# Attention stage written out lap by lap: scores two sequences ahead, value products between score steps, split of the maxima on GpSimd, second LayerNorm applied on ScalarE, two row buffers

## The reference, cut to what matters

```python
h = _layernorm(x, ln1_g, ln1_b)
qkv = h @ w_qkv + b_qkv
q, k, v = jnp.split(qkv, 3, axis=-1)          # each [B, S, H=16, DK=8]
scores = jnp.einsum('bqhd,bkhd->bhqk', q, k) / np.sqrt(DK)
attn = jax.nn.softmax(scores, axis=-1)
o = jnp.einsum('bhqk,bkhd->bqhd', attn, v).reshape(B, S, D)
x = x + o @ w_o + b_o
h = _layernorm(x, ln2_g, ln2_b).reshape(B * S, D)
logits = h @ gate_w + gate_b
topv, topi = jax.lax.top_k(logits, TOPK)
```

## Time and profile before

| | |
|---|---|
| median of three runs | 776.5 us (772.96 to 779.0) |
| the profiled execution, its own time | 773.37 us |
| its span, first to last instruction | 771.5 us |
| mean granted clock of TensorE | 0.901 of full speed |
| busy in the span: TensorE, DVE, POOL, ScalarE | 79%, 66%, 57%, 49% |

### The profile page before, as it was taken

How to read it: one execution, slowest core, us unless ns; L and a number is a source line. 1 busy time by engine, 2 the same in 40 slices (tenths; PEclk the granted TensorE clock), 3 DMA queues, 4 the chain that set the end, 5 groups by cost and what they waited for, 6 DMA issues and landing times. The chain is left out here.

```text
span 771.5 us, 19028 instructions
## 1 busy us (share of the span) xinstructions
PE 607.2 (79%) x5634; PEld 494.0 (64%) x5634; DVE 512.3 (66%) x1558; ACT 379.7 (49%) x796; POOL 436.2 (57%) x524
## 2 busy tenths in 40 slices
PE   3999936999992887379999899999931499999950
PEld 1556625989991554246777666667621499999950
DVE  2655544766762889546789678788654378778735
ACT  1543403655560444337777767767511355556520
POOL 2477761766776576342436575576476055666650
PEclk9999977999995699759999999999975699999985
DMA  5921146766754279313443353355214798888519
GB/s 166 255 69 48 52 101 170 216 199 199 220 154 125 74 217 272 121 38 96 91 111 91 81 134 86 85 130 118 40 40 98 240 292 257 244 253 243 174 40 325
DMA packets 97817, 115.03 MB, mean 149 GB/s; under 512 B 16128, under 2 KB 77600, under 8 KB 97632
## 3 DMA queue, kind: packets, MB, share of 16 engines
q1 hardware_dynamic: 82224, 92.36, 44.0%
q0 software_dynamic: 9088, 18.76, 7.7%
q10 hardware_dynamic: 6448, 3.20, 1.7%
HBM read 80.75 MB, written 33.53 MB: 148 GB/s over the span
## 5 line engine op out<-in xcount | busy, mean ns | idle before, releaser
L403 POOL DMA_INDIRECT dispatch_rows<-row,index x128 | 127.5, 996 | 86.3 <-DVE index L384 51.0
L765 POOL DMA_INDIRECT expert_rows<-fo,to x78 | 84.0, 1077 | 67.0 <-DVE fo L1804 53.5
L1501 DVE TENSOR_REDUCE mneg<-ps 128x4 f32<-128x512 f32 x128 | 86.8, 690 | 42.3 <-PE ps L1619 40.2
L765 POOL DMA_INDIRECT expert_rows<-eo,to x78 | 75.0, 962 | 48.5 <-ACT eo L858 25.6
L1593 ACT ACTIVATE prob<-ps 128x512 f32<-128x512 f32 x128 | 76.3, 598 | 51.4 <-PE ps L1628 45.7
L738 DVE CAST xh<-psT 128x256 fp32r<-128x256 f32 x78 | 33.1, 425 | 73.2 <-PE psT L706 71.5
L1619 PE MATMUL ps<-km,qp 96*128 96x512 f32 x128 | 58.4, 459 | 23.3 <-POOL km L1453 17.0
L1793 PE MATMUL psO<-wb,fh 128*128 128x128 f32 x624 | 75.9, 275 | 0.0
L1793 PEld LDWEIGHTS psO<-wb,fh 128*128 128x128 f32 x624 | 73.1, 192 | 0.0
L756 PE MATMUL psA<-xh,wh 128*128 128x256 f32 (+1 forms) x234 | 73.0, 312 | 0.0
L1453 POOL TENSOR_SCALAR km<-kp,const 96x512 fp32r<-96x512 f32 x32 | 52.6, 1644 | 24.8 <-DMA kp<-qk_parts 18.7
(11 more groups left out here) (200 smaller groups left out, 1549.5 us busy)
## 6 DMA issues: line engine op xcount, KB each, us to landing
wb<-in_W1b SPq DMA_DIRECT2D x39, 578.0 KB
w<-in_W SPq DMA_DIRECT2D x39, 304.0 KB
qk_parts<-qk SPq DMA_DIRECT2D x8, 1024.0 KB, 5.0
qp<-qk_parts SPq DMA_DIRECT2D x48, 128.0 KB, 3.2
kp<-qk_parts SPq DMA_DIRECT2D x48, 128.0 KB, 3.5
qm<-qk_parts SPq DMA_DIRECT2D x192, 32.0 KB
xs<-dispatch_rows SPq DMA_DIRECT2D x39, 130.0 KB
xt<-dispatch_rows SPq DMA_DIRECT2D x39, 130.0 KB
```

Source lines behind the costliest of these rows:

```text
L403: pool.indirect_dma_start(out=m.xbuf, out_offset=bass.IndirectOffsetOnAxis(ap=r.index[b][:, c:c + 1], axis=0), in_=r.row[b][:, c // TOPK, ...
L765: pool.indirect_dma_start(out=m.ybuf, out_offset=bass.IndirectOffsetOnAxis(ap=to[b][:, a:a + 1], axis=0), in_=out[b][:, a, :], in_offset=N ...
L1501: ins = nc.vector.tensor_reduce(mneg[p][:, g, :], ps1[:, g % 2, :].rearrange("p (j k) -> p j k", j=4), AX_X, ALU.max, negate=True)
```

## The change

`attention` and its `post_*` steps are written out as straight code for all sequences, in laps s from 0 to 45; the work of a group n lies in fixed laps after 4n (`group(s, after)`).

- Scores: eight for sequences 0 and 1 come first, then lap s holds `score(s + 2)` beside `shift(s)`; `mix(s - 1)` and `total(s - 1)` are cut in two halves each, one behind each group g. `turn_max(s + 1)` stands behind g = 1, `project(s - 2)` behind g = 2.
- Masks of the keys: three sequences are made first, then lap s ends with `mask_k(s + 3)` on ScalarE, behind the fourth exponential. There are still two `km` buffers, and three of `qp` and `kp`.
- The split of the maxima (`part_max`) is done by POOL, at the head of a lap.
- The second LayerNorm: DVE makes -mean times rstd (`post_centre`), ScalarE applies it, between the third and the fourth exponential of its lap.
- The router's steps on DVE are cut in single operations between the maxima. The last groups use the same banks as the others. The two row buffers alternate (n % 2), and two rows' DMAs go out in each of the laps 4n + 10 to 4n + 13, four at a time before.
- The semaphore `spare` is joined with `tails`.

The diff, cut to its core; what it takes out of the streams is printed above.

```diff
+def post_centre(q, dve, n):
 
     dve.wait_ge(q.rooted, n + 1)
-    wait(dve, q.turned, n)
+    wait(dve, q.normed, n)
+    q.m.nc.vector.scalar_tensor_tensor(out=q.offset[:], in0=q.mv[:, :, 0], scalar=-1.0, in1=q.rstd[:],
+                                       op0=ALU.mult, op1=ALU.mult).then_inc(q.centred, 1)
+
+
+def post_normalise(q, act, n):
+
+    act.wait_ge(q.centred, n + 1)
+    wait(act, q.turned, n)
     for t in range(GT):
-        ins = q.m.nc.vector.tensor_scalar(q.norm[:, t, :], post_stream(q, n, t), q.mv[:, t, 0:1],
-                                             q.rstd[:, t:t + 1], ALU.subtract, ALU.mult)
+        ins = q.m.nc.scalar.activation(q.norm[:, t, :], post_stream(q, n, t), ACT.Identity,
+                                       bias=q.offset[:, t:t + 1], scale=q.rstd[:, t:t + 1])
...
+        LAPS = SEQS + 14
+
+        def group(s, after):
+
+            n, rest = divmod(s - after, GT)
+            return n if rest == 0 and 0 <= n < GROUPS else None
...
+                for k in range(PAIRS):
+                    if k >= 2:
+                        if k >= PAIR_BUFFERS:
+                            sp.wait_ge(shifted, HG * 2 * (k - PAIR_BUFFERS + 1))
+                        load_pair(m, sp, k, k % PAIR_BUFFERS)
+                    if k < 2:
+                        sp.wait_ge(zeroed[k], 1)
+                    else:
+                        sp.wait_ge(shifted, HG * 2 * (k - 1))
...
+                def part_max(s):
+                    p = s % 2
+                    pool.wait_ge(maxed, HG * (s + 1))
+                    wait(pool, turned, s - 1)
+                    x = xm[p][:]
+                    hi, lo = (bass.AP(x.tensor, x.offset + w, [list(x.ap[0]), [32, HG], [130, 4]]) for w in range(2))
+                    nc.gpsimd.tensor_copy(hi.bitcast(F32R), mneg[p][:]).then_inc(link, 1)
+                    pool.wait_ge(link, s + 1)
+                    nc.gpsimd.tensor_tensor(lo, mneg[p][:], hi, ALU.subtract).then_inc(parted, 1)
...
+                mask_k(0)
+                mask_k(1)
+                nc.gpsimd.memset(qm[1][:].bitcast(F32), 0.0).then_inc(zeroed[1], 1)
+                for b in range(2):
+                    nc.gpsimd.memset(xm[b][:], 0.0)
+                    nc.gpsimd.memset(vb[b][:], 0.0).then_inc(cleared, 1)
+                nc.gpsimd.memset(post.minus_half[:], -0.5)
+                pool.wait_ge(cleared, 2)
+                part_max(0)
+                mask_k(2)
+                for s in range(LAPS):
+                    if s + 1 < SEQS:
+                        part_max(s + 1)
+                    if s + 3 < SEQS:
+                        mask_k(s + 3)
+                    if s < SEQS:
+                        spread_v(s)
+                    n = group(s, 6)
+                    if n is not None:
+                        post_root(post, pool, n)
+                    for part in range(GT):
+                        n = group(s, 10 + part)
+                        if n is not None:
+                            post_scatter(post, pool, n, n % 2, range(TOPK * part, TOPK * (part + 1)))
+                    n = group(s, 8)
+                    if n is not None:
+                        post_join(post, pool, n)
...
+                for s in range(LAPS):
+                    inner = 2 <= s < SEQS + 2
+                    varying, centring, routing, placing = (group(s, k) for k in (6, 7, 9, 10))
+                    if s + 2 < SEQS:
+                        maximum(s + 2, 0)
+                    if varying is not None:
+                        post_moments(post, dve, varying, kept)
+                    if centring is not None:
+                        post_centre(post, dve, centring)
+                    if inner:
+                        invert(s - 2)
+                    if routing is not None:
+                        post_logits(post, dve, routing, routing % 2, post.natural_banks)
+                    if s + 2 < SEQS:
+                        maximum(s + 2, 1)
+                    if varying is not None:
+                        post_gather(post, dve, varying)
+                    if placing is not None:
+                        index_slot(r, dve, placing, post.rank_out)
+                    if inner:
+                        divide(s - 2)
+                    if routing is not None:
+                        choose_best(r, dve, routing)
+                    if s + 2 < SEQS:
+                        maximum(s + 2, 2)
+                    if varying is not None:
+                        post_variance(post, dve, varying)
+                    if routing is not None:
+                        choose_expert(r, dve, routing)
+                    if placing is not None:
+                        index_place(r, dve, placing, post.rank_out)
+                    if s + 2 < SEQS:
+                        maximum(s + 2, 3)
+                    if routing is not None:
+                        choose_hot(r, dve, routing)
+                    if placing is not None:
+                        index_sum(r, dve, placing)
+                    if inner:
+                        keep(s - 2)
+                    if routing is not None:
+                        choose_mask(r, dve, routing)
...
+                for s in range(3):
+                    mask_k(s)
+                copy_max(0)
+                for s in range(LAPS):
+                    norming, scaling, routing = (group(s, k) for k in (7, 8, 9))
+                    if s < SEQS:
+                        exponent(s, 0)
+                    if scaling is not None:
+                        post_scale(post, act, scaling)
+                    if routing is not None:
+                        post_rows(post, act, routing, routing % 2, routing // 2, post.natural_banks)
+                    if s < SEQS:
+                        exponent(s, 1)
+                    if s + 1 < SEQS:
+                        copy_max(s + 1)
+                    if s < SEQS:
+                        exponent(s, 2)
+                    if norming is not None:
+                        post_normalise(post, act, norming)
+                    if s < SEQS:
+                        exponent(s, 3)
+                    if s + 3 < SEQS:
+                        mask_k(s + 3)
+                    if routing is not None:
+                        post_rows_again(post, act, routing, routing % 2)
+                        post_weigh(post, act, routing, routing % 2)
...
+                for s in range(2):
+                    for g in range(HG):
+                        score(s, g)
+                pe.wait_ge(cleared, 3)
+                turn_max(0)
+                for s in range(LAPS):
+                    behind, inner = 1 <= s < SEQS + 1, 2 <= s < SEQS + 2
+                    turning, scaling, routing, placing = (group(s, k) for k in (7, 8, 9, 10))
+                    for g in range(HG):
+                        if s + 2 < SEQS:
+                            score(s + 2, g)
+                        if s < SEQS:
+                            shift(s, g)
+                        if behind:
+                            (mix if g < 2 else total)(s - 1, (2 * (g % 2), 2 * (g % 2) + 1))
+                        if g == 0 and placing is not None:
+                            wait(pe, kept, min(s - 2, SEQS))
+                            pe.wait_ge(post.nat_copied, placing + 1)
+                            pe.wait_ge(post.router.got, placing + 1)
+                            post_rank(post, pe, placing, placing % 2, post.rank_out)
+                        if g == 1 and s + 1 < SEQS:
+                            if scaling is not None:
+                                pe.wait_ge(post.hT_done, scaling + 1)
+                            if routing is not None:
+                                pe.wait_ge(post.nat_copied, routing + 1)
+                                pe.wait_ge(post.router.got, routing + 1)
+                            turn_max(s + 1)
+                        if g == 2 and inner:
+                            if routing is not None:
+                                pe.wait_ge(post.nat_copied, routing + 1)
+                                pe.wait_ge(post.router.got, routing + 1)
+                            if placing is not None:
+                                pe.wait_ge(post.router.slotted, placing + 1)
+                            project(s - 2)
+                    if turning is not None:
+                        wait(pe, mxT_done, min(s + 2, SEQS))
+                        wait(pe, post.nat_copied, turning)
+                        wait(pe, post.router.got, turning)
+                        post_turn(post, pe, turning)
+                    if scaling is not None:
+                        wait(pe, kept, min(s - 1, SEQS))
+                        wait(pe, mxT_done, min(s + 2, SEQS))
+                        wait(pe, post.router.slotted, scaling)
+                        post_natural(post, pe, scaling, post.natural_banks)
```

(72 more changed lines are left out.)

346 lines of the change are left out of this document (102 added, 244 removed).

## The result

The changed kernel takes 856.7 us (median of 4 runs, 850.4 to 861.6) where the kernel before takes 776.9 on the same chip: a ratio of 1.101, interval 1.096 to 1.105. It is 10% slower. The forecast was 834 us, slower, with a range of 804 to 862.

The account below looks back on a forecast made before the run. Bound: TensorE's work and a ScalarE loop (last shift, exponential, masks, next score), the latter about to lose its cover. Profiled 773.4 + 49.6 (laps, earlier start) - 10 (tail) + 21 (clock) = 834 us, range 804 to 862.

Parts of the forecast that it names:

- The lap, 8.4 us: Plain attention lap, first score to next first score: 8.4 us instead of 5.9, TensorE idle about 2.3 us at its end.
- The way: TensorE's stretch from a lap's first score to its last shift: 5.07 to 5.51 us, taken as 5.3.
- Router and LayerNorm, 8 us: Router and second LayerNorm steps inside laps: 1.4 us for each of nearly six groups, 8 us.
- my row: Profile row of two 128x128 ScalarE activations in 0.63 us, from which four normalisations were put at 1.2 us.
- DVE and POOL at nothing: Neither engine bounds laps of 8.4 us; POOL's two added small operations, 0.5 us per sequence, cost the lap nothing.
- First to last shift without the clock: Attention stretch at held clock: 29 laps, three last laps, router steps and slow start sum to 270.6 us, before 220.
- The clock, 21 us: TensorE's clock halves after idle lap ends: 13.5 laps hit, 1.55 us each, 21 us; bounds none and 45 us.
- Rival (2): Clock falls in nearly every lap, also those with router work: 45 us for the clock, 858 us in all; chance 0.09.
- Rival (1): TensorE's clock holds in spite of the idle lap ends: 813 us; chance 0.20.
- Rival (3): TensorE's own work, not the masks, paces the laps: 6.4 us per lap, 747 us; chance 0.06.
- Tail, -10 us: After the last shift: last accumulation at about 7 us instead of 17.1, the end about 10 us sooner.
- Start, -1 us: Start of the attention stage: first shift about 1 us sooner, since POOL starts with the masks, not the memsets.

Follow-up runs that it names:

- Experiment 1: The changed kernel with ScalarE's three key masks one by one between the exponentials and pair loads ahead of mask-query loads: 773.5 us, ratio 0.989.
- experiment 2: The changed kernel with value products, projection and sums put back behind the last shift, masks still late: 791.2 us, ratio 1.015.
- experiment 4: The changed kernel with 128x128 matmuls nobody reads (seven, four or none) at the end of each lap: 824.5 us, ratio 1.057.
- experiment 7: The changed kernel with the second LayerNorm's normalisation back on DVE, run on the slower second chip: 919.5 us, ratio 1.053.
- experiment 6: The changed kernel with the split of the maxima back on DVE, run on the slower second chip: 926.7 us, ratio 1.062.
- experiment 12: The changed kernel with masks early, pair loads ahead, products in two blocks and the normalisation back on DVE: 753.7 us, ratio 0.971.
- first batch: The chip on which the masks-early, cover-put-back, products-alone and idle-matmul runs were made; the kernel before took 779.4 us there.
- experiment 5: The changed kernel with two of the four key masks on POOL instead of one, on the slower second chip: 892.9 us, ratio 1.022.
- experiment 3: The kernel before with only value products and sums cut in halves and moved between its score and shift steps: 886.5 us, ratio 1.137.
- experiments 8 and 11: One kernel on two chips: the changed kernel with masks early, pair loads ahead, products in two blocks: 829.3 us (ratio 0.951) and 758.7 us (0.974).

## Why the prediction was right, and where it missed

**What bounds the kernel.** Right. The loop through ScalarE, last shift, exponential, three masks, next first score, kept its length (3.16 us before, 3.10 or 2.95 after). Experiment 1 shortened it and the loss went; experiment 2 covered it and most of the loss went.

**The lap, 8.4 us.** Right in size. Without the low clock (experiment 4) plain laps take 8.6 on average. The way in that experiment is 5.57 us (first score 388.07, last shift 393.64), just outside the bounds of 5.07 and 5.51 from which the sum took 5.3. A block of score and shift took 0.87 to 0.91 us there, above the upper price of 0.83, and a half set of narrow matmuls 0.57 instead of 0.51; the transposes took 0.41 instead of 0.58 and the projection 0.25 instead of 0.31. A tail that is 2.95 in every other lap makes up for the rest. With the router steps the forecast had 8.75 per lap on average; 35.15 us for four laps is 8.79.

**Router and LayerNorm, 8 us.** The sum was somewhat high: the 35.15 us are 0.8 more than four plain laps of 8.6, where the forecast had 1.4 a group. Its parts did not all: four normalisations took 1.64 us, not 1.2. The Trainium skill, page "ScalarE: Activation LUTs", section "What ACT_TABLE_LOAD costs", was nearer than my row: an estimate from its sum, 0.39 us each in a row of them, makes 1.56 for four. My nearest row had other operands. On the path it cost nothing that experiment 7 could show.

**DVE and POOL at nothing.** Right. The two small operations took 0.21 and 0.23 us, 0.44 in all against 0.5, and in experiment 6 taking them away brought nothing that can be seen.

**First to last shift without the clock: forecast 270.6, experiment 4 has 269.5.**

**The clock, 21 us.** This is the term that was mis-sized: it measured 35.7 us, 15 more. Its price for a fall was nearly right: laps of 10.0 against 8.6 us are 1.45, forecast 1.55. The count was wrong: 17 single and three double patches are 23, where the forecast took 13.5; with the double one in the slow start the 84 us of low clock that experiment 4 took away are 24.6 times 3.4, and 24.6 times 1.45 is 35.7. Two choices made the count low. I let only three in four of the long waits count, with one case to go by, and nearly every one was followed by a fall; and I left the laps with normalised transposes (forecast idle 1.7) out of the count, while all six waits of 1.79 or 1.80 us in them were followed by one (457.65). Rival (2), the clock falling nearly always, had 45 us, and the truth lies between, nearer to it. That its total, 858, is closer to the measured 856.7 than my 834 is partly luck: its clock term is 9 us too high, and the later start and the earlier stages, which no forecast had in its sum, make up for it.

**Rival (1), the clock holds, 813 us.** Wrong. The Trainium skill, page "TensorE: Matmul & The Clock Gate", section "Why this matters for your kernels", warns only of idle gaps longer than these; here gaps of 1.79 to 2.24 us in most laps brought the lower level, and the measurement decides.

**Rival (3), TensorE paces the lap, 747 us.** Not what the change did. It asked for a shorter tail, and experiment 1 made one, but its price for TensorE's work was too low: it kept 5.93 us for a plain lap and had 6.4 with the router steps on average, where experiment 1 has 6.5 and 7.2, and 219.2 us in the stretch instead of 205. Only with the narrow matmuls in two blocks, experiment 12, are plain laps 5.83, laps on average 6.7 and the stretch 202.9.

**Tail, -10 us.** Right: last accumulation 7.1 us after the last shift (654.11), forecast 7; 10.4 us won.

**Start, -1 us.** Wrong: +1.0. The first split of the maxima is now POOL's, and I had not looked at what is queued ahead of it there:

```profile
325.81 7.52 POOL L1515 TENSOR_SCALAR km<-kp,const 96x512 fp32r<-96x512 f32 x2 [12.96 <-POOLq L1052]
333.29 3.50 POOL L1540 MEMSET qm<- 96x4096 f32 x1
...
338.65 0.20 POOL L1525 CAST xmx<-mneg 128x16 fp32r<-128x16 f32 x1
```

The masks come sooner, the split only behind every memset: 12.8 us into the stage, where DVE's began at 9.9 (331.56 in the kernel before). Another 4.2 us were there before the stage began, in stages whose work the change doesn't touch. It is not only the difference of two executions: the two traces with the old attention code have this start at 321.6 and 323.7 us, all eight with the new code on the chips of like speed at 324.9 to 331.2, and on the first batch's chip it is 323.7 against 329.9 to 331.2. What delays it stays open.

**Sum.** 15 for the clock, 2 for the start and 4 for the earlier stages make the 21 us between 834 and the profiled 855; the median is 2 more. Direction and mechanism were right, the size of the clock term was not, and that the time lay inside the range rests on its upper end having been set by rival (2).

## What to carry to other kernels

When work is moved, ask what it was covering: here 2.9 us of matmuls stood under a chain of 3.1 us on another engine. Most of them were moved away from under it, and the lap grew by all that was moved, 2.4 us, by 0.4 for the wide matmuls that now stand between narrow ones, and by the clock on top. Where a chain of waits ends in work that has idle time earlier in the lap, move that work before touching the cover; the masks between the exponentials turned +10% into nothing measurable (+0.4%), with the pair loads issued earlier into -1%, and with the products in two blocks instead of four into -3%. And when a wait goes, look at what it hid: here a wait of 1.9 us for a load in one lap of four, worth 16 us.

## What the runs showed of the hardware

- In the changed kernel the granted clock fell to 0.50 at 20 of 22 idle times of TensorE between 1.79 and 2.24 us, for 3.25 to 7 us, and 1.83 us of matmuls that nobody needs kept it at 1.00. Idle time alone doesn't decide. Two of the longest had no fall behind them (2.15 and 2.24 us), and in experiment 6 there were 16 falls for 22 such idle times. In experiment 5 none of 1.18 and 1.38 us had one, and one of three of 1.53 us did. In experiment 3, whose laps with router work have two or three waits each, falls came with idle times of 1.31 us (363.55) and 1.37 us (466.10). What else decides is open.
- Each change to a block of 32-column matmuls and back to wide ones cost TensorE some 0.23 us beyond the matmuls. Two steps of score and shift with one block each take 2.92 us in experiment 4 (388.07 to 390.99), the same work with one double block 2.69 us in experiment 12 (361.54 to 364.23). Two fewer such blocks make 0.5 of the 0.7 us by which grouping shortened the plain lap; the other 0.2 are not explained.
- The kernel before took 776.9 to 779.4 us on three occasions and 868.7 on a fourth, another chip. Of the kernels traced there, the same one as on another chip (experiments 8 and 11) had 214.0 and 208.0 us from first to last shift, and reached its first score at 385.2 and 332.3 us: most of the time was lost in the stages ahead.
